# Leaf numbers of two of three routing trees: transposed on the tensor engine, or spread over the partitions by DMA

## What is computed

```python
def _fff(x, nw, nb, w1, b1, w2, b2, act):
    node = zeros
    for _ in range(8):
        logit = einsum('bsd,bsd->bs', x, nw[node]) + nb[node]
        node = 2 * node + 1 + (logit > 0)
    leaf = node - 255
    h = act(einsum('bsd,bsdl->bsl', x, w1[leaf]) + b1[leaf])     # 16 wide
    return einsum('bsl,bsld->bsd', h, w2[leaf]) + b2[leaf]
...
q, k, v = _fff(xn2, q...), _fff(xn2, k...), _fff(xn2, v...)       # relu
y = xn2 + softmax(q @ k.T / sqrt(128)) @ v
ffn = y + _fff(y, f...)                                            # gelu
```

## Time and profile before

| | us |
|---|---|
| median of 3 runs | 660.62 (658.90 to 664.24) |
| the profiled execution, its own time | 660.97 |
| its span, first to last instruction | 659.2 |
| PE busy in the span | 581.6 (88%) |
| DVE busy | 411.2 (62%) |
| ACT busy | 351.5 (53%) |
| POOL busy | 273.0 (41%) |

### The profile page before, as it was taken

How to read it: one execution, slowest core, us unless ns; L and a number is a source line. 1 busy time by engine, 2 the same in 40 slices (tenths; PEclk the granted TensorE clock), 3 DMA queues, 4 the chain that set the end, 5 groups by cost and what they waited for, 6 DMA issues and landing times.

```text
span 659.2 us, 11736 instructions
## 1 busy us (share of the span) xinstructions
PE 581.6 (88%) x3641; PEld 407.7 (62%) x3641; DVE 411.2 (62%) x966; ACT 351.5 (53%) x742; POOL 273.0 (41%) x288
## 2 busy tenths in 40 slices
PE   2499888999999999999999999988598988988985
PEld 0344465868686878777766656765165666665643
DVE  3856587576666666666666655666866665646730
ACT  4533333655555646465665645523155878785633
POOL 7852676770757842840058100000077800002860
PEclk9999999999999999999999999988689999989989
DMA  7979968785768884886422100000043755531230
GB/s 211 258 170 192 318 166 227 210 218 148 218 185 218 174 203 127 193 181 158 129 36 36 26 1 0 1 1 1 1 116 68 154 146 143 139 104 41 35 70 16
DMA packets 108701, 83.05 MB, mean 126 GB/s; under 512 B 8680, under 2 KB 105840, under 8 KB 108640
## 3 DMA queue, kind: packets, MB, share of 16 engines
q1 hardware_dynamic: 93344, 69.68, 40.4%
q0 software_dynamic: 15104, 12.63, 10.4%
q10 hardware_dynamic: 192, 0.00, 0.0%
HBM read 57.91 MB, written 24.36 MB: 125 GB/s over the span
## 4 chain that ended last, share of the span: by engine, by line
PE 68%; ACT 10%; DVE 9%; issue 6%; DMA 3%; POOL 2%; SPq 2%; DVEq 0%; ACTq 0%
PE ps L1129 9%; PE ps L1141 8%; PE ps L1131 8%; PE ps L1118 7%; PE ps L1195 6%; PE ps L1205 6%; PE ps L1066 4%; DVE ps L707 3%; PE ps L1015 2%; POOL xs L426 2%; PE ps L1248 2%; PE ps L1262 2%; PE ps L1189 2%; PE ps L1200 2%; ACT hr L887 2%
## 5 line engine op out<-in xcount | busy, mean ns | idle before, releaser
L707 DVE CUSTOM_DVE_ANT_0 ps<-ps,strip 128x512 f32<-128x512 f32 x256 | 177.5, 699 | 111.4 <-PE ps L1118 107.0
L876 ACT ACTIVATE pt<-ps 128x512 f32<-128x512 f32 x256 | 150.5, 600 | 100.1 <-PE ps L1131 97.5
L1129 PE MATMUL ps<-qs,km 128*128 128x512 f32 x256 | 129.0, 504 | 7.9 <-ACT pt L876 6.9
L1118 PE MATMUL ps<-km,qs 128*128 128x512 f32 x256 | 110.8, 436 | 9.1 <-DVE mx L707 7.7
L431 POOL DMA_INDIRECT yt<-ys,slot x48 | 74.6, 1554 | 80.1 <-DMA ys<-yl 66.1
L887 ACT ACTIVATE hr<-ps,wt 128x128 f32<-128x128 f32 x192 | 54.9, 369 | 65.7 <-PE ps L1195 65.6
L1131 PE MATMUL ps<-u_lo,rev_r 128*128 128x220 f32 (+1 forms) x256 | 75.2, 294 | 0.0
L1131 PE MATMUL ps<-u_hi,rev_r 128*128 128x220 f32 (+1 forms) x256 | 73.8, 288 | 0.0
L1129 PEld LDWEIGHTS ps<-qs,km 128*128 128x128 f32 x256 | 49.7, 194 | 35.1 <-ACT pt L876 21.9
L426 POOL DMA_INDIRECT xs<-xr,slot x64 | 62.7, 979 | 19.7 <-issue 18.3
L1141 PE MATMUL ps<-pt,v_aug 128*32 128x512 f32 x512 | 69.9, 619 | 0.7 <-ACT pt L876 0.7
(11 more groups left out here) (232 smaller groups left out, 890.6 us busy)
## 6 DMA issues: line engine op xcount, KB each, us to landing
wt<-in_wl SPq DMA_DIRECT2D x192, 128.5 KB
xl<-xs SPq DMA_DIRECT2D x48, 258.0 KB, 3.9
ys<-yl SPq DMA_DIRECT2D x48, 256.0 KB, 3.2
xs<-mx SPq DMA_DIRECT2D x2, 3096.0 KB, 22.8
strip<-bias_bf SPq DMA_DIRECT2D x1, 3584.0 KB, 38.8
u_hi<-bias_hi SPq DMA_DIRECT2D x1, 2496.0 KB, 17.3
u_lo<-bias_lo SPq DMA_DIRECT2D x1, 2496.0 KB, 30.0
xs<-xr,slot POOLq DMA_INDIRECT x64
```

Of the source, the lines that this page charges most:

```text
L707: V.tensor_tensor_reduce(out=bank(u % 2), in0=bank(u % 2), in1=strip[:, HG * g + j, b0:b0 + NS], scale=1.0, scalar=LOWEST, op0=ALU.add, op ...
L876: A.activation(pt[:, kt % 2, j, :], bank(2 + u % 2), ACT.Exp).then_inc(S["ex"], 1)
L1118: T.matmul(bank(u % 2), qs[:, par, qt * P:(qt + 1) * P], backward(km[:, par, j, :]), start=True, stop=True).then_inc(S["p1"], 1)
L1129: T.matmul(bank(2 + u % 2), km[:, par, j, kt * P:(kt + 1) * P], qs[:, par, :], start=True, stop=False)
```

## The change

For the second and the third tree (groups 12 to 35, `by_row`) the four transposes of stage m are gone. The leaf numbers take another way:
- GpSimd, after the scatter of a tree's rows, converts the leaf numbers to bf16 and scatters them with 16 more indirect DMAs, one 2-byte number per partition and DMA, into a row of DRAM in sorted order (`leaf_row`, one for each of the two trees). The row is zeroed at the start by one more small DMA from SP for each.
- SP loads for each such group its 512 numbers, 1 KB, into all 128 partitions with one DMA (`leaves`), into one buffer `leaf_at` that lies in `b_pT`. It waits for `hm` of the group before.
- DVE's `hm` waits for this DMA (`d_at`) instead of `mk`, and reads the numbers from SBUF as bf16 instead of from PSUM as f32.
- SP loads the rows of group n+2 as soon as x of group n is through (`xT`) instead of waiting for `mk`.
- PE's wait for `yl` of the group before moves to stage y.
The first and the fourth tree keep their transposes.

```diff
--- before.py
+++ after.py
@@ -76,6 +76,16 @@
 ATT_PE, ATT_DVE, ATT_ACT = {"s": 0, "p": 2, "o": 3}, {"s": 0, "o": 3}, {"s": 1, "p": 2}
+def by_row(n):
+
+    return GROUPS <= n < NTREE * GROUPS
+
+
+def spread_before(n):
+
+    return n if n < GROUPS else n - (NTREE - 1) * GROUPS
+
+
 def slot_of(n, at):
     return n * SLOTS + at
@@ -119,6 +129,7 @@
     bias_lo = nc.dram_tensor("bias_lo", [H, 2 * NS], F32).ap()
     bias_bf = nc.dram_tensor("bias_bf", [H, 2 * NS], BF16).ap()
     xs = [nc.dram_tensor(f"xs{t}", [TILES * P, ROW], F32).ap() for t in range(2)]
+    leaf_row = [nc.dram_tensor(f"leaf_row{t}", [TILES * P, 1], BF16).ap() for t in range(1, NTREE)]
     ys = [nc.dram_tensor(f"ys{t}", [TILES * P, P], F32).ap() for t in range(NTREE)]
     ctx = ExitStack()
@@ -177,6 +188,7 @@
         st = sb("st", [P, 8, NT])
         whole = sb("whole", [P, BLK], I32)
         part_of = sb("part_of", [P, NTREE + 1, NT], I32)
+        part_bf = sb("part_bf", [P, NT], BF16)
         ewc = sb("ewc", [P, NTREE + 1], I32)
         sm = sb("sm", [P, 5, BLK])
@@ -188,6 +200,7 @@
         path_bf = b_pT[:].bitcast(BF16)
         paths = path_bf[:, 0:2 * LEAVES].rearrange("p (h l) -> p h l", h=2)
         blks = path_bf[:, 2 * LEAVES:2 * LEAVES + 2 * (BLK + 2)].rearrange("p (h l) -> p h l", h=2)
+        leaf_at = path_bf[:, 0:GT * P]
         bitsT = flat(yt[:, 2]).bitcast(BF16).rearrange("p (h t) -> p h t", h=2)
         leafT = flat(yt[:, 0]).bitcast(BF16).rearrange("p (h t) -> p h t", h=2)
         nw_f, nb_f = flat(xTs[:])[:, 0:NODES], flat(xTs[:])[:, NODES:2 * NODES]
@@ -215,7 +228,7 @@
         bank = lambda i: ps[:, i, :]
         S = {n: ctx.enter_context(nc.semaphore(n)) for n in (
-            "d_ew0 d_ew1 d_ew2 d_ew3 d_x d_c d_w d_u d_b d_f d_z d_n d_sc tc pa oh hb pop nbt d_nb z_mx pl tab_in d_far aug lkc mxc "
+            "d_ew0 d_ew1 d_ew2 d_ew3 d_x d_c d_w d_u d_b d_f d_z d_n d_sc tc pa oh hb pop nbt d_nb d_sl d_at z_mx pl tab_in d_far aug lkc mxc "
             "sl tick rt_in rt_out ones ln_m ln_r ln_sub ln_sq ln_out xT_ps xT_sb xnT_sb tab_ps tab_sb v_ps v_sb lg bit oh5 rk rt id wsc "
             "proj p1 mt p2 pv ot at pr h ex osb ats vr qs ks km max qs2 rc norm acc "
             "lx0 lx1 lw0 lw1 st xT xTs hh hr mk hm yy yl d_nf yT_ps yT_sb "
@@ -249,6 +262,9 @@
             for t in range(2):
                 sp.dma_start(xs[t].rearrange("(p a r) c -> p a (r c)", p=P, r=n),
                              zeros).then_inc(S["d_z"], 16)
+            for row in leaf_row:
+                sp.dma_start(row.rearrange("(p a) one -> p (a one)", p=P), flat(mx[:]).bitcast(BF16)[:, 0:TILES]
+                             ).then_inc(S["d_z"], 16)
             sp.wait_ge(S["tab_sb"], 3)
@@ -276,6 +292,13 @@
                 for k, e in enumerate(block_of):
                     sp.dma_start(wt[:, par, k, :], wl[bass.ds(e, 1), :, :].rearrange("a p c -> p (a c)")).then_inc(LW_[par], 16)
+            def leaves(n):
+
+                t, m = divmod(n, GROUPS)
+                sp.wait_ge(S["d_sl"], 16 * NT * t)
+                sp.dma_start(leaf_at, bass.AP(tensor=leaf_row[t - 1].tensor, offset=m * GT * P, ap=[[0, P], [1, GT * P]])
+                             ).then_inc(S["d_at"], 16)
+
             def turn(n, last):
                 if n + 2 < last:
@@ -283,9 +306,15 @@
                     if (n + 2) % GROUPS == 0:
                         sp.wait_ge(S[f"d_ew{t}"], 16)
                         sp.wait_ge(S["d_sc"], 16 * NT * (t + 1))
-                    sp.wait_ge(S["mk"], n + 1 + CREDIT["mk"])
+                    sp.wait_ge(S["xT"], n + 1)
+                    if not by_row(n):
+                        sp.wait_ge(S["mk"], spread_before(n) + 1 + CREDIT["mk"])
                     rows(n + 2)
                     block_of = blocks(n + 2)
+                if by_row(n + 1):
+                    sp.wait_ge(S["hm"], n + 1 + CREDIT["hm"])
+                    leaves(n + 1)
+                if n + 2 < last:
                     sp.wait_ge(S["yy"], n + 1 + CREDIT["yy"])
                     weights(block_of, n % 2)
                 t, m = divmod(n, GROUPS)
@@ -412,7 +441,7 @@
                 settle(G.memset(left[:].rearrange("p a b -> p (a b)"), -1.0))
                 settle(G.affine_select(left[:], left[:], [[-P, KT], [P, KT - 1]], ALU.is_ge, 0.0,
                                        base=P - SAT - 1, channel_multiplier=-1))
-                pool.wait_ge(S["d_z"], 32)
+                pool.wait_ge(S["d_z"], 16 * (2 + len(leaf_row)))
                 for k in range(2 * HG):
                     c = HR * (k // 2) + 25 + 3 * (k % 2)
                     G.tensor_copy(mx[:, :, c:c + 3], left[:]).then_inc(S["mxc"], 1)
@@ -420,12 +449,21 @@
             def scatter(t):
                 pool.wait_ge(S["sl"], t + 1)
                 if t >= 2:
-                    pool.wait_ge(S["mk"], GROUPS * (t - 1) + CREDIT["mk"])
+                    pool.wait_ge(S["xT"], GROUPS * (t - 1))
+                    pool.wait_ge(S["mk"], GROUPS + CREDIT["mk"])
                 settle(G.tensor_copy(xr[:, :, P], part_of[:, t, :]))
                 for k in range(NT):
                     pool.indirect_dma_start(out=xs[t % 2][:, :], out_offset=bass.IndirectOffsetOnAxis(ap=slot[:, t, k:k + 1], axis=0),
                                             in_=xr[:, k, :], in_offset=None).then_inc(S["d_sc"], 16)
                 pool.wait_ge(S["d_sc"], 16 * NT * (t + 1))
+
+            def scatter_leaves(t):
+
+                settle(G.tensor_copy(part_bf[:], part_of[:, t, :]))
+                for k in range(NT):
+                    pool.indirect_dma_start(out=leaf_row[t - 1][:, :], out_offset=bass.IndirectOffsetOnAxis(ap=slot[:, t, k:k + 1], axis=0),
+                                            in_=part_bf[:, k:k + 1], in_offset=None).then_inc(S["d_sl"], 16)
+                pool.wait_ge(S["d_sl"], 16 * NT * t)
             def fetch(dst, src, idx, op, done):
                 pool.indirect_dma_start(out=dst, out_offset=None, in_=src[:, :],
@@ -458,10 +496,12 @@
             left_rows()
             scatter(0)
             scatter(1)
+            scatter_leaves(1)
             pool.wait_ge(S["id"], NTREE)
             gather_b2(0)
             gather_b2(1)
             scatter(2)
+            scatter_leaves(2)
             gather_b2(2)
             for t in range(NTREE):
                 gather(t)
@@ -733,10 +773,13 @@
             def stage(k, n):
                 if k == "m":
-                    dve.wait_ge(S["mk"], n + 1 + CREDIT["mk"])
+                    if by_row(n):
+                        dve.wait_ge(S["d_at"], 16 * (n - GROUPS + 1))
+                    else:
+                        dve.wait_ge(S["mk"], spread_before(n) + 1 + CREDIT["mk"])
                     dve.wait_ge(S["hr"], n + 1 + CREDIT["hr"])
                     dve.wait_ge(S["yy"], n + CREDIT["yy"])
-                    V.scalar_tensor_tensor(flat(hm[:]), bank(BB[k]), col(C_LEAF), flat(hr[:]), ALU.is_equal, ALU.mult
+                    V.scalar_tensor_tensor(flat(hm[:]), leaf_at if by_row(n) else bank(BB[k]), col(C_LEAF), flat(hr[:]), ALU.is_equal, ALU.mult
                                            ).then_inc(S["hm"], 1)
                 elif k == "y":
                     dve.wait_ge(S["yy"], n + 1 + CREDIT["yy"])
@@ -796,7 +839,7 @@
                     add_out(b)
             dve.wait_ge(S["d_u"], 48)
-            dve.wait_ge(S["d_z"], 32)
+            dve.wait_ge(S["d_z"], 16 * (2 + len(leaf_row)))
             for at in range(SLOTS):
                 if at >= LAG:
                     row_max(0, 0, at - LAG)
@@ -1194,6 +1237,8 @@
                     for i in range(GT):
                         last = T.matmul(quarter(BB[k], i), wt[:, par, i, 0:P], xTs[:, i, :], start=True, stop=True)
                     last.then_inc(S["hh"], 1)
+                elif k == "m" and by_row(n):
+                    pass
                 elif k == "m":
                     pe.wait_ge(S["yl"], n + CREDIT["yl"])
                     for i in range(GT):
@@ -1201,6 +1246,7 @@
                     last.then_inc(S["mk"], 1)
                 else:
                     pe.wait_ge(S["hm"], n + 1 + CREDIT["hm"])
+                    pe.wait_ge(S["yl"], n + CREDIT["yl"])
                     for i in range(GT):
                         last = T.matmul(quarter(BB[k], i), hm[:, i, :], wt[:, par, i, P:2 * P], start=True, stop=True)
                     last.then_inc(S["yy"], 1)
```

## The result

The changed kernel takes 669.98 us (median of 4 runs, 665.71 to 672.99) beside 662.43 for the kernel before on the same chip (4 runs, 658.90 to 666.05). The ratio is 1.0123, with a 95% interval of 1.0083 to 1.0163: slower by about 8 us, and outside the range forecast. The ratios are estimated over the executions that no slow state disturbed and are not the quotients of the medians beside them (here that would be 1.0114).

The account below looks back on a forecast made before the run. PE's list looked full, but the prediction held that PE meets ACT's or DVE's results late, transposes filling the wait. Terms -2.0 - 0 + 0 + 0.8 = -1.2 us gave a median of 659.4 us, range 654.0 to 667.2.

Parts of the forecast that it names:

- Part 1: PE in groups 12 to 35: removing 96 transposes, 10.6 us of PE time, gains 2.0 us of program time.
- slot 3: Groups 14, 19, 24, 29, 34: x stage already starts 0.11 us after hr, the signal's time, so gain 0.
- all that stands in the chain is gained: Rival: all 19 transpose pieces of 0.44 us in the chain of waits count, 8.4 us, giving 652.2 us; chance 0.13.
- slot 7: Groups 15, 20, 25, 30: x stage starts 0.38 us after hr, 0.27 free, gain 4 x 0.27 = 1.1 us.
- slot 11: Groups 16, 21, 26, 31: x stage starts 0.33 us after hr, 0.22 free, gain 4 x 0.22 = 0.9 us.
- Part 2: DVE's hm reading SBUF instead of PSUM: gain between 0 and 0.3 us, taken as 0.
- the stretching by GpSimd: Rival: GpSimd's work slows each of 24 hm on DVE by 201 ns, 4.8 us, giving 664.2 us; chance 0.06.
- Part 3: GpSimd's 32 leaf scatters: 47 us of its list with landing waits, covered by 84.5 us of its waiting; cost 0.
- Part 4: SP's longer turn and DVE's wait for the leaf load: +0.8 us for ten tight turns, ends 0 and 4.5.
- The rival on the slower side: Rival: DVE's hm waits for a leaf load landing in 4.6 us, ten turns late by 1.15 us, 670 us; chance 0.15.

Follow-up runs that it names:

- Bare: Changed kernel without the zeroing, scatters and loads of leaf numbers, transposes still gone, masks of two trees uncomputed: 0.9949 of the kernel before, repeated 0.9976.
- two_no_scatter: Changed kernel with two leaf-number buffers, loads issued by SP one group earlier, without the 32 leaf scatters (masks wrong): 657.76 us, 0.9969 of the kernel before.
- two_buffers: Changed kernel, complete, with the leaf load issued by SP one group earlier into two buffers used alternately: 664.28 us, 1.0061 of the kernel before.
- load_only: Changed kernel without the 32 leaf scatters; one buffer, SP's loads read a zeroed row (masks wrong): 661.75 us, 1.0026 of the kernel before.
- tiny_issue: Bare plus one 8-byte DMA per SP turn at the leaf load's place, which nobody waits for: 658.74 us, 0.9982 of the kernel before.
- act_loads: Changed kernel, complete, with two buffers and the leaf loads issued by ACT behind its y slot instead of by SP: 661.22 us, 1.0030 of the kernel before.
- act_again: Repeat of act_loads, unchanged, timed beside the kernels with an early second scatter: 662.04 us, 1.0040 of the kernel before.
- narrow_scatter: Bare plus GpSimd's 32 leaf scatters of 2 bytes per partition, no zeroing, no leaf loads: 661.25 us, 1.0010 of the kernel before.
- narrow_again: Repeat of narrow_scatter, unchanged, in another set of runs: 656.30 us, 0.9964 of the kernel before.

## Why the prediction was wrong

The forecast was 659.4 against 660.62, a difference of -1.2 us. It is about +7.5 us.

**Part 1, -2.0 us: right.** Bare is 2.5 us below before on average of two. x follows `hr` by 0.11 us at slot 3, the gain is a quarter to a third of the PE time removed, and the rival "all that stands in the chain is gained" (8.4 us) is excluded. In the profile the gain is 3.4 us, and it arises where the forecast said, behind slots 7 and 11: the distance from one `hm` to the next is shorter than before by 0.38 to 0.41 us each time behind slot 7 and by 0.32 to 0.33 behind slot 11 (forecast 0.27 and 0.22), and by 0.06 or less elsewhere. Why each is about 0.1 us larger than worked out was not tested.

**Part 2, 0: right.** `hm` from SBUF takes 750 ns, like `hm` from PSUM:

```profile
L782 DVE SCALAR_TENSOR_TENSOR hm<-b_pT,cst,hr 128x512 f32<-128x512 bf16 x24 | 18.0, 750 | 17.7 <-DMA b_pT<-leaf_row 9.7 <-ACT hr L930 8.0
```

The 57 ns that L641 suggested are not there, nor is the stretching by GpSimd: that rival is refuted, although GpSimd was busy 106.74 of 175 us. The rule of the Trainium skill behind it (GPSIMD Engine Reference, Key points), contention for two SBUF inputs, does not show in this instruction: its 24 executions took 747 to 757 ns.

**Part 3, GpSimd's scatters cost 0: the failed step.** The argument looked at GpSimd's list alone, and for that it was right. A scatter of 2 bytes takes 979 ns on average, as one of 516 bytes does (979), and GpSimd's last long wait shrank from 46.95 to 35.33 us (forecast 37):

```profile
341.96 1.54 POOL L469 DMA_INDIRECT yt<-ys,slot  x1 [35.33 <-DMA ys<-yl]
```

What it left out is what 2048 writes of 2 bytes into one row of 12 KB do to the other queues: in most profiles some landing comes late by some 3 us once or twice and PE stands. The runs put this at about 2 us without leaf loads (within the spread of their repeats), 3.8 us with loads on ACT (early against late; the intervals at most touch, and nothing but the scatter is moved), and 5 to 6 us with loads from SP (0.92% between two_no_scatter and two_buffers, 0.75 and 0.97% between load_only and the two measurements of the changed kernel). In the changed kernel's own two profiles the mechanism is seen only weakly: one store wait of 2.39 us in the second, none as long in the first, and no fall of the clock. They are 2.5 and 3.8 us longer from group 11 to 35 than load_only. That adding the scatters to these loads costs time is shown; how they do it in the changed kernel is inferred from its relatives.

**Part 4, +0.8 us: the second failed step, right in kind, too small.** The place was named (DVE's wait for the load, in ten groups), its upper end was 4.5 us at a landing of 3.9, and the row of the same shape gave 3.3. The 0.8 us did not follow from the working beside it: with a margin of 0.15 us at a landing of 3.3 even the tight turns would not have been late. The load took 3.4 us in the median and 4.2 at most without the scatters (load_only), 3.7 and 5.7 with them, 3.4 in the repeat. The Trainium skill's figure of 2 us for an HBM access at high load (DMA: Bandwidth & Descriptors, Latency and other measured facts) gave an estimate of 3.3 to 5.1 us; the landings here spread from 2.9 to 5.7, with the median near its low end. The single buffer costs 3.8 us (5.0 in the profiles). The error was to price a load in a stretch that runs at 72% of the queues by one row from another time, although the rows' 3.9 us stood beside it. SP's fuller list costs about 1 us as long as nothing behind it is urgent (0.9 in the profile of tiny_issue, 0.2 in that of two_no_scatter).

**The sum as measured:** -2.5 for the transposes, up to +1 for the list and the bytes, +3.8 for the late load, +5 to 6 for the scatters in its company: +6 to +8, beside +7.5 measured. This is a division and not a check: the terms are the steps of one chain of kernels, from bare over two_no_scatter and load_only to the changed kernel, so they must come out near the whole. Each is the difference of two ratios with intervals of 0.24 to 0.52% to either side, that is 1.6 to 3.4 us. In another order they would differ: the scatter's term is 2 us without loads and 5 to 6 beside them. The rival on the slower side had the first of the two mechanisms (670 us, at a landing of 4.6) and was given 0.15. Its number came out by luck: by less of its own mechanism than it asked for (a median landing of 3.7, ten waits of 1.0 us on average) and by one that stood nowhere.

## What to carry to other kernels

When a step moves from an engine to DMA, price three things apart: the engine time freed (here a quarter to a third of it was time), the landing in the stretch where it will be used, with a second buffer if that landing is near the moment of use, and what the new traffic does to transfers that were in time until now. Element-sized scatters into a dense row may belong ahead of the stretch whose queues are full: this gained 0.5 to 0.6% in the version with two buffers and ACT's loads, and nothing in the two others. And before an engine list is called idle cover, look at which other list shares its queues.

## What the runs showed that was not expected

- Beside indirect scatters of 2 bytes into a dense row, stores and weight loads of other queues landed late in 9 of 11 profiles. That it is the density is suggested and not shown: the same 2-byte writes 512 bytes apart had no late landing between 115 and 230 us and 0.9951, and 516-byte writes none and 0.9978, at 258 times the bytes. This rests on one profile and 12 runs each, and two of the eleven profiles with dense scatters have none either.
- In two_buffers a window in which PE worked 1.41 of 4 us was followed by one at a granted clock of 0.50; there a late landing was paid twice. The clock fell likewise between 208 and 220 us in act_loads, act_again and narrow_scatter, but not in narrow_again, nor in either profile of the changed kernel.
- An 8-byte DMA added to each of SP's turns raised the waits for stores from 3.4 us to 16.2 in the touched stretch, and the time by 0.4 to 2 us. SP's list was near its pace: with the four register loads between a row load and the next issue (207.31 to 210.68 in the changed kernel), a turn has little to spare at 6.84 us per group.
